# Row statistics of two layer norms taken by ScalarE in the stage in front, instead of by VectorE at the head of the norm's own stage

## The reference, cut to what matters

```
def _layernorm(x, axis=-1, eps=1e-05):
    m = jnp.mean(x, axis=axis, keepdims=True)
    v = jnp.var(x, axis=axis, keepdims=True)
    return (x - m) / jnp.sqrt(v + eps)
...
xn = _layernorm(x, axis=-1)
x = x + _L1_attn_ref(xn) + _L1_ffn_ref(xn, ...)
xn = _layernorm(x, axis=-1)
x = x + _L2_attn_ref(xn, ...) + _L2_ffn_ref(xn, ...)
```

## Time and profile before

| | |
|---|---|
| median of 3 timed runs | 2124.78 us (2124.61 to 2125.85) |
| profiled execution, its own time | 2104.8 us |
| its span | 2102.9 us |
| TensorE busy | 1800.2 us (86%) |
| VectorE busy | 1394.7 us (66%) |
| ScalarE busy | 740.2 us (35%) |
| GpSimd busy | 578.4 us (28%) |
| mean granted clock of TensorE | 0.925 |

### The profile page before, as it was taken

The page is one execution under the profiler, slowest core; times in us unless marked ns, Lnnn a source line. Parts: engine busy times, 40 slices in busy tenths (PEclk is TensorE's granted clock), DMA queues, the critical chain, the costliest instruction groups (busy, mean ns, idle before and its releaser), DMA issues. The chain is left out here.

```text
span 2102.9 us, 37015 instructions
## 1 busy us (share of the span) xinstructions
PE 1800.2 (86%) x13832; PEld 1433.3 (68%) x13832; DVE 1394.7 (66%) x2980; ACT 740.2 (35%) x1733; POOL 578.4 (28%) x550
## 2 busy tenths in 40 slices
PE   5844189944999999999999997999988997989995
PEld 2432177833899999999899985455566875767773
DVE  5588255548787777777787775666656777644444
ACT  2424134422333343434333333145534323322221
POOL 1326735540121221212221112622232103511111
PEclk9976699975999999999999997989998996999998
DMA  9448244443000000000000100000001007111114
GB/s 324 142 132 269 88 136 146 149 150 111 1 1 24 24 2 24 1 24 1 24 1 24 34 1 1 0 1 2 2 1 53 29 1 251 62 43 48 49 49 140
DMA packets 103060, 134.86 MB, mean 64 GB/s; under 512 B 11628, under 2 KB 78984, under 8 KB 102376
## 3 DMA queue, kind: packets, MB, share of 16 engines
q1 hardware_dynamic: 91800, 102.01, 15.5%
q0 software_dynamic: 11088, 30.49, 4.0%
HBM read 81.92 MB, written 50.54 MB: 63 GB/s over the span
## 5 line engine op out<-in xcount | busy, mean ns | idle before, releaser
L1138 POOL TENSOR_TENSOR a_rstd<-a_msq,consts 128x8 f32<-128x8 f32 x32 | 52.4, 1636 | 556.2 <-DVE a_msq L1493 556.2
L110 PE MATMUL a_ring<-a_w_hi,l_xnT_hi 128*128 128x256 f32 x512 | 152.0, 297 | 0.0
L110 PE MATMUL a_ring<-a_w_hi,l_xnT_lo 128*128 128x256 f32 x512 | 144.6, 282 | 0.0
L110 PE MATMUL a_ring<-a_w_lo,l_xnT_hi 128*128 128x256 f32 x512 | 144.4, 282 | 0.0
L2487 POOL DMA_INDIRECT l_slots_in<-xn,f_row_of x96 | 105.2, 1096 | 82.0 <-DVE f_row_of L2815 37.0
L3048 POOL DMA_INDIRECT l_pairs_out<-f_yb,f_to_row x96 | 94.6, 985 | 97.6 <-ACT f_yb L3023 70.9
L1450 DVE RECIPROCAL a_rT<-a_rT 128x256 f32<-128x256 f32 x64 | 111.5, 1744 | 0.0
L1739 PE MATMUL b_ring<-b_keys,b_qm 32*128 32x128 f32 (+2 forms) x896 | 94.2, 347 | 14.9 <-DVE b_nm L1952 9.4
L1905 ACT ACTIVATE b_work<-b_ring 128x1024 f32<-128x1024 f32 (+1 forms) x96 | 81.1, 881 | 65.1 <-PE b_ring L1746 64.1
L2942 PE MATMUL f_pgu<-f_gate_up_w,f_xT 128*128 x384 | 95.0, 391 | 5.5 <-ACT f_xT L3003 5.4
L1739 PEld LDWEIGHTS b_ring<-b_keys,b_qm 32*128 32x128 f32 x896 | 67.1, 198 | 46.4 <-issue 23.4
(11 more groups left out here) (514 smaller groups left out, 5359.6 us busy)
## 6 DMA issues: line engine op xcount, KB each, us to landing
l_slots_in<-l_zeros SPq DMA_DIRECT2D x4, 3120.0 KB, 22.2
f_xb<-l_slots_in SPq DMA_DIRECT2D x11, 1040.0 KB, 5.7
f_gate_up_w<-l_pairs_out SPq DMA_DIRECT2D x16, 512.0 KB, 8.7
l_slots_in<-l_zeros SPq DMA_DIRECT2D x3, 1690.0 KB, 19.0
f_xb<-l_slots_in SPq DMA_DIRECT2D x39, 130.0 KB, 2.1
f_down_w<-L_ffn_w_down_dram SPq DMA_DIRECT2D x1, 4096.0 KB
f_gate_w<-L_ffn_w_dram SPq DMA_DIRECT2D x2, 2048.0 KB, 11.1
f_up_w<-L_ffn_w_dram SPq DMA_DIRECT2D x2, 2048.0 KB, 19.7
```

The costliest lines, as they stand in the source:

```text
L110: ins = pe.matmul(out, a, b, start=start and k == 0, stop=stop and k == 2, **kw)
L1138: pool.tensor_tensor(rstd[:], msq[:], core.consts[:, C_HALF:C_HALF + 8], ALU.pow).then_inc(s["rstd_ready"], 1)
```

## The change

Both norms get `ahead=core.row_stats`. With it the statistics operations of VectorE at the head of `p1` and `n2` are gone. In their place ScalarE takes them at the end of `j0` and `f1`, for two tiles at a time, as soon as VectorE has added to both: the sum of a row (Copy with an accumulator), minus a sixteenth of the mean and minus the mean (two small operations on two columns), and the sum of squares of x/16 less mean/16 (Square with a bias and an accumulator). GpSimd adds epsilon and raises to -0.5, the first half at the end of `j0` and `f1`, the second half at the head of `p1` and `n2`. The four numbers of a row stand in its four spare words. The result that is written per element goes into `xn`, which nobody reads before it is overwritten.

```diff
+class RowStats:
+    def __init__(self, marks):
+        self.total, self.minus_16th, self.minus, self.var = (marks[:, :, k] for k in range(4))
+        self.rstd = self.minus_16th
+
+    def tiles(self, act, core, first, n, step, done):
+        cols = slice(first, first + n)
+        for t in range(first, first + n):
+            ins = act.activation(core.xn[:, t, :], core.x[:, t, :], ACT.Copy, accum_out=self.total[:, t:t + 1])
+        step(ins)
+        step(act.activation(self.minus_16th[:, cols], self.total[:, cols], ACT.Copy, scale=-1.0 / (16 * D)))
+        act.activation(self.minus[:, cols], self.total[:, cols], ACT.Copy, scale=-1.0 / D)
+        for t in range(first, first + n):
+            ins = act.activation(core.xn[:, t, :], core.x[:, t, :], ACT.Square, bias=self.minus_16th[:, t:t + 1],
+                                 scale=1.0 / 16, accum_out=self.var[:, t:t + 1])
+        ins.then_inc(done, 1)
+
+    def power(self, pool, core, half, eps, step, done):
+        n = TILES // 2
+        cols = slice(half * n, (half + 1) * n)
+        step(pool.tensor_scalar(self.var[:, cols], self.var[:, cols], eps, None, ALU.add))
+        pool.tensor_tensor(self.rstd[:, cols], self.var[:, cols], core.consts[:, C_HALF:C_HALF + n], ALU.pow
+                           ).then_inc(done, 1)
...
     def tile_row(self, dve, t):
+        if self.ahead is not None:
+            if t == TILES // 2:
+                dve.wait_ge(self.rstd_ready, 1)
+            dve.tensor_scalar(self.row_of(t), self.src[:, t, :], self.ahead.minus[:, t:t + 1],
+                              self.ahead.rstd[:, t:t + 1], ALU.add, ALU.mult).then_inc(self.rows_ready, 1)
+            return
...
     def vector(self, dve):
         for part in range(self.parts):
-            self.part_stats(dve, part)
+            if self.ahead is None:
+                self.part_stats(dve, part)
...
     def gpsimd(self, pool):
+        if self.ahead is not None:
+            self.ahead.power(pool, self.core, 1, self.eps, Steps(pool, self.shift_step), self.rstd_ready)
+            return
...
 # layer0_join, scalar
+            step = Steps(act, s["act_step"])
+            for t in range(0, TILES, 2):
+                act.wait_ge(s["added"], t + 2)
+                core.row_stats.tiles(act, core, t, 2, step, s["squared"])
 # layer0_join, gpsimd
+            pool.wait_ge(s["squared"], HALF // 2)
+            core.row_stats.power(pool, core, 0, 1e-5, Steps(pool, s["pool_step"]), s["powered"])
...
 # slots_experts, scalar
+            for g in range(GROUPS):
+                act.wait_ge(s["added"], 2 * K * (g + 1))
+                core.row_stats.tiles(act, core, 2 * g, 2, step, s["squared"])
```

More of the change, by code:

```diff
@@ L212, in __init__ @@
     def __init__(self, st, core, src, tok_out, out_T, eps, rms=False, gain=None, shift=None, also_load=None, ring=4,
-                 turned=None, parts=2, row=None, banks=None):
+                 turned=None, parts=2, row=None, banks=None, ahead=None):
+        self.ahead, self.shift_step = ahead, st.sem("shift_step")
         self.core, self.src, self.tok_out, self.out_T, self.eps, self.rms = core, src, tok_out, out_T, eps, rms
@@ L216, in __init__ @@
         self.PER = TILES // parts
-        self.raw = st.sb("raw", [P, TILES, 6])
-        self.mean, self.var, self.rstd = (st.sb(n, [P, TILES]) for n in ("mean", "var", "rstd"))
+        if ahead is None:
+            self.raw = st.sb("raw", [P, TILES, 6])
+            self.mean, self.var, self.rstd = (st.sb(n, [P, TILES]) for n in ("mean", "var", "rstd"))
         if tok_out is None and row is None:
@@ L375, in __init__ @@
     def __init__(self, st, core, src, tok_out, dst, eps, w):
-        Normalise.__init__(self, st, core, src, tok_out, None, eps, also_load=w.load_first)
+        Normalise.__init__(self, st, core, src, tok_out, None, eps, also_load=w.load_first, ahead=core.row_stats)
         self.dst, self.w, self.hi_out = dst, w, st.sem("hi_out")
     def vector(self, dve):
-        for part in range(self.parts):
-            self.part_stats(dve, part)
         for t in range(TILES + self.BEHIND):
@@ L729, in layer0_join @@
     sums, ff = st.ps("sums", [P, SLOTS, 512]), st.ps("ff", [P, SLOTS, 512])
-    names = "diag_ready sums_back ff_back rows_copied x_added y_ready stats dve_step var_ready rstd_ready gained added".split()
+    names = ("diag_ready sums_back ff_back rows_copied x_added y_ready stats dve_step var_ready rstd_ready gained "
+             "added act_step squared pool_step powered").split()
     s = {n: sem(n) for n in names}
@@ L2893, in slots_experts @@
     names = ("x_turned x_copied gu_ready setup_step limits_ready biased clipped silu_ready h_ready h_turned h_copied "
-             "y_ready y_copied rows_step rows_found cw_turned cw_copied bias_ready bias_added added").split()
+             "y_ready y_copied rows_step rows_found cw_turned cw_copied bias_ready bias_added added "
+             "act_step squared pool_step powered").split()
     s = {n: sem(n) for n in names}
@@ L3049, in _ @@
                                             yb[:, i % YR, j, :], None).then_inc(stored[i % YR], 16)
+            pool.wait_ge(s["squared"], GROUPS // 2)
+            core.row_stats.power(pool, core, 0, 1e-5, Steps(pool, s["pool_step"]), s["powered"])
         @block.vector
@@ L3545, in build @@
         core.xn, core.marks = core.rows[:, :, 0:D], core.rows[:, :, D:ROW]
+        core.row_stats = RowStats(core.marks)
         core.consts = resident("consts", [P, C_END])
```

3 lines of the change are left out of this document (2 added, 1 removed).

## The result

The changed kernel took 2130.6 us (median of 9 runs, 2128.1 to 2133.1), and the kernel before, beside it, 2125.5: a ratio of 1.003, with a 95% interval of 1.0021 to 1.0038. It is 5.1 us slower. The prediction was 2121.8 us, 3.0 us faster, so the prediction was off by 8 us against the same base, and on the wrong side.

A forecast was written before the change was run, and what follows sets the result against it. VectorE's statistics were taken to hold the heads of `p1` and `n2` for 7.94 and 7.93 us. Path to `f1` +0.6, path to `a2` -3.6: -3.0 us from 2124.78 gives 2121.8, range 2118.8 to 2125.5.

The forecast's parts named there:

- GpSimd's half is done long before: End of `f1`: GpSimd's operations on the first half of the statistics finish early and add nothing to the tail.
- +2.3 us: End of `f1`: ScalarE keeps up with VectorE, so only its last pair shows behind the last addition, 2.3 us.
- the 5.55 us in which GpSimd is idle ahead of `f1`: Before `f1`: GpSimd's shortest idle of any engine, taken to show that the block begins when GpSimd has sent its rows.
- p, the time of a pair: ScalarE's statistics for two tiles: 2.2 us a pair, bounds 2.0 to 3.06, counted eight times in the sum.
- the tail is 7.5 and not 7.0: End of `j0`: ScalarE falls behind VectorE's 1.58 us a pair, so the barrier comes 7.0 us later.
- The head of `p1`: Start of `p1`: rows start 7.88 us sooner, and a wait for the router's loads takes 1.5 us back.
- The stop behind the third tile: In `p1`: TensorE stands 1.5 us waiting for the router's bias load, bounds 0 to 2.0.
- Routing, sends and `f1` move along: `p1` to `f1`: later work shifts with VectorE's chain, its length unchanged; path to `f1` +0.6 us.
- only GpSimd's sends end the stage: End of `p1`: `f1` begins once GpSimd has sent its rows; the weights do not hold it back.
- The head of `n2`: Start of `n2`: -7.88 us, less a 2.0 us wait of ScalarE for weights; block some 5.9 us shorter.
- Rival 2: End of `j0`: ScalarE's slots do not overlap behind a wait, so the kernel is slower; over +4.25 us, chance 0.06.
- Rival 3: Only `n2` pays: something else times `f1`, `p1` loses another 1 to 3 us; -2 to 0 in all, chance 0.12.

The follow-up runs named there:

- e5_gpsimd_last: The kernel before, with GpSimd after its sends in `f1` waiting for VectorE's last addition and then clearing an unread 128x8 scratch: 2111.61 us, ratio 1.0041.
- e6_n2_drained: The change for `n2`'s norm alone, plus one GpSimd drain right behind its last scattered send in `f1`, against the kernel before: 2097.79 us, ratio 0.9977.
- e1_before_again: The kernel before, unchanged, run and profiled once more: 2124.93 us, ratio 1.0003.
- e11_add_early: The kernel before, with GpSimd in `f1` draining after its sends, then adding 1e-5 to 128x8 numbers beside VectorE's additions: 2101.46 us, ratio 0.9997.

## Why the prediction was wrong

**The step that failed** is at the end of `f1`: "GpSimd's half is done long before", and with it the term "+2.3 us" for the whole tail. ScalarE's last pair was indeed 2.4 us behind the last addition. But GpSimd was not done long before: its addition of epsilon got no turn until VectorE's additions ended, so that its power ended at 514.07, half a microsecond ahead of ScalarE's last read. And the step left out what comes behind GpSimd's last instruction, the drain, which ends 7.9 us later. Before, it was over 24 us ahead of the last addition. Now it was open for 7.4 us more (9.19 + 2.40 - 1.74 = 9.85 us more between the last addition and the next block, less the 2.4). `e5_gpsimd_last` shows the cost without the change, `e6_n2_drained` takes it away. The trace of before held the row for it, in the view of the block's opening line. The prediction even quoted the effect of one such drain, the 5.55 us in which GpSimd is idle ahead of `f1`, and read it as the end of the sends.

**The whole in the profile.** Against `e1_before_again`, and counted from VectorE's last addition in `j0`, the changed kernel's `f1` begins 1.2 us later, is 1.8 us longer (231.90 against 230.09), has 9.85 us more behind it, and `n2` is 6.1 us shorter: +6.7 us, where -3.0 was predicted and +5.1 (4.5 to 8.1) measured. The drain is 7.4 us of the difference.

**p, the time of a pair.** 2.2 predicted; in the changed kernel's profile the pairs of `j0` start every (135.27 - 121.74) / 6 = 2.26 us. The slots are as built, but seven times 0.06 is 0.4 us, and the tail is 7.5 and not 7.0. That the last read ended at 137.62, with 137.7 predicted, is partly luck: VectorE's additions lay 0.5 us earlier in that profile.

**The head of `p1`.** The stop behind the third tile was there; its price was mis-sized. 1.5 us predicted, 2.0 measured with the clock that rises later, and 0.4 more without it. The scores came 5.4 us sooner behind the block's start (10.0 against 15.4 in `e1_before_again`), and not 6.4. The term that the prediction put at nothing is TensorE's clock.

**"Routing, sends and `f1` move along."** The first send did, though with +2.1 and not +0.6 us. `f1` did not quite: with the routing's norm changed it is 1.1 to 1.9 us longer inside, cause open. By the profiles of the shorter kind this makes some 3 us of cost for this half in place of 0.6; the timed runs say 2.5 and 2.9, each within 2 us. It was also wrong that only GpSimd's sends end the stage. In the shorter profiles it is their drain, and in the longer ones GpSimd is idle for 13 to 15 us ahead of `f1` and the attention ends last.

**The head of `n2`.** 5.9 us predicted, 6.1 measured, with the wait of 1.87 at its place. Right.

**The rivals.** Rival 2, the way to slower, was a tail of ScalarE at `j0`. The tail was 0.5 us longer than predicted, which is far from enough; the sign came from a mechanism that was on no list. Rival 3 had `p1` losing 1 to 3 us more, by way of the sends; the size is about right, the place is not. The range, 2118.8 to 2125.5, came from the bounds of the listed terms alone, and so had no room for it.

## What to carry to other kernels

Before you give an engine work at the end of a block, look at its drain there, in the view of the block's own line, and compare its end with the end of the engine's last operation. Behind GpSimd's scattered sends that difference was 5.3 to 7.9 us in this layer, and an instruction that ends less than this ahead of the block's last work lays it open. Either let that engine have no work behind its sends, or drain right behind them, where other work hides it. Nor did a GpSimd operation that reads SBUF get a turn while VectorE added back to back, so what waits for it comes later still. And where a producer outruns the engine that takes the statistics, give that engine only the tiles that it finishes under cover, and leave the rest where it was. Half the tiles in both places gave 7 us, and half in `j0` with all 16 and the early drain in `f1` gave as much. All of them lost 5, and gave nothing even with the drain moved.

## What the runs showed of the hardware

- GpSimd's drain ends 7.9 us behind its last operation in `f1` (96 scattered sends since the last drain), right behind the sends (`e1_before_again`) and after 32 us of idling (`e5_gpsimd_last`: 489.72 to 497.65), and 5.3 us behind the 64 sends of `p1`. Once a drain had run, the next ended within 0.1 us of GpSimd's last work (`e11_add_early`: 22.3 us from 463.7, ending with the probe). That is 0.08 us a send in both blocks, but layer 3 of the kernel before has 1.8 us behind 4 sends and 3.3 behind 39, and no run varied the number, so what the figure depends on is open.
- A GpSimd addition on 128x8 took 0.26 us at the head of `n2` and 0.38 at that of `p1`, 1.55 beside VectorE's spaced operations in `j0`, 10.29 and 22.18 us beside back-to-back `scalar_tensor_tensor`, ending 0.11 us behind them both times.
- The same kernel took 2102 us in two batches and 2122 to 2125 in two others, nearly all of the difference in layer 1's attention and experts; behind the start of `a2`, the rest of the span is 1587.3 to 1590.6 us in all of them.
